# Second edge sort of a graph network kernel: one fp32 product per edge column becomes two 16-bit products

## The reference, cut to what matters

```python
src = src[_o]; dst = dst[_o]                  # 50000 edges
x = x + _L0_gnn_ref(_layernorm(x, axis=-1), L0_gnn_W, src, dst, edge_weight)
# inside: h = einsum('nd,od->no', x, W); msgs = edge_val[:, None] * h[edge_col]
#         out = segment_sum(msgs, edge_row, num_segments=N_NODES)
```

## Time and profile before

| | |
|---|---|
| median of 3 runs | 6542.18 us (6538.23 to 6543.29) |
| profiled execution, first to last instruction (span) | 6540.4 us |
| profiled execution, own time | not listed apart from the span |
| phase "a" with the second sort | about 467 to 1027 us |
| PE / DVE / ACT / POOL busy over the span | 79% / 53% / 38% / 26% |
| mean granted TensorE clock | 0.884 |

### The profile page before, as it was taken

How to read it: one execution, slowest core, us unless ns; L and a number is a source line. 1 busy time by engine, 2 the same in 40 slices (tenths; PEclk the granted TensorE clock), 3 DMA queues, 4 the chain that set the end, 5 groups by cost and what they waited for, 6 DMA issues and landing times. The chain is left out here.

```text
span 6540.4 us, 90176 instructions
## 1 busy us (share of the span) xinstructions
PE 5198.6 (79%) x22747; PEld 3549.0 (54%) x22748; DVE 3445.6 (53%) x7515; ACT 2507.4 (38%) x5926; POOL 1683.8 (26%) x1619
## 2 busy tenths in 40 slices
PE   6939998999796999997999679494656666646886
PEld 3516664444485777766788557273323444333576
DVE  9837777877654444435000244514369899855111
ACT  7947774666321000001223100131355666531343
POOL 5877771000022000001011300045334444310012
PEclk9979998999898999998999889797757777778888
DMA  1113333333263222221156432075324444430055
GB/s 30 23 17 100 102 101 106 150 150 153 105 201 111 72 71 71 72 76 39 50 188 199 148 100 66 23 211 159 120 57 130 133 131 135 118 100 2 27 158 171
DMA packets 407400, 682.31 MB, mean 104 GB/s; under 512 B 72738, under 2 KB 304300, under 8 KB 406732
## 3 DMA queue, kind: packets, MB, share of 16 engines
q1 hardware_dynamic: 328540, 489.55, 23.4%
q0 software_dynamic: 74192, 186.38, 10.5%
q10 hardware_dynamic: 4512, 4.46, 0.2%
HBM read 510.90 MB, written 169.02 MB: 104 GB/s over the span
## 5 line engine op out<-in xcount | busy, mean ns | idle before, releaser
L1683 POOL DMA_INDIRECT e_xb<-table,source x188 | 180.7, 961 | 2351.1 <-issue 1894.4
L1099 DVE TENSOR_TENSOR a_diff<-a_cu 128x640 f32<-128x640 uint16 x480 | 396.0, 825 | 627.5 <-PE a_pa L1137 627.5
L995 PE MATMUL ty_pc<-ty_ohr,ty_ohl 128*128 128x512 bf16 (+1 forms) x3416 | 662.5, 357 | 2.5 <-DVE ty_ohl L934 2.5
L2570 POOL DMA_INDIRECT mx_at_rows<-heads,mx_at_ix x416 | 483.1, 1161 | 622.3 <-PE mx_at_pa L2616 519.0
L1137 PE MATMUL a_pa<-a_diff,y_sb 128*128 128x320 f32 (+1 forms) x2000 | 548.4, 434 | 63.8 <-DVE a_diff L1106 63.8
L1640 ACT ACTIVATE e_h<-e_phid,e_b 128x256 f32<-128x256 f32 (+1 forms) x760 | 332.5, 438 | 688.0 <-PE e_phid L1598 670.2
L1661 DVE TENSOR_TENSOR e_ys<-e_py,e_bl 128x256 f32<-128x256 f32 x188 | 79.9, 425 | 968.3 <-PE e_py L1610 968.3
L969 ACT CAST ty_new<-ty_pc 128x512 uint16<-128x512 f32 x854 | 449.1, 541 | 266.6 <-PE ty_pc L995 266.6
L1598 PE MATMUL e_phid<-e_xt,e_w 128*128 128x256 f32 (+1 forms) x2800 | 524.0, 345 | 2.9 <-ACT e_xt L1628 2.9
L1610 PE MATMUL e_py<-e_wl,e_h 128*128 128x256 f32 x2288 | 512.4, 379 | 0.0
L995 PEld LDWEIGHTS ty_pc<-ty_ohr,ty_ohl 128*128 128x128 bf16 x3416 | 314.3, 98 | 350.7 <-DVE ty_ohl L934 4.2
(11 more groups left out here) (599 smaller groups left out, 8947.5 us busy)
## 6 DMA issues: line engine op xcount, KB each, us to landing
counts<-ty_snap SPq DMA_DIRECT2D x122, 800.0 KB
a_cu<-counts SPq DMA_DIRECT2D x500, 160.0 KB
mx_work<-bc SPq DMA_DIRECT2D x160, 320.0 KB, 3.6
e_w<-in_L_ffn_W SPq DMA_DIRECT2D x33, 1024.0 KB
e_wl<-in_L_ffn_W SPq DMA_DIRECT2D x32, 1024.0 KB
e_wl<-in_L_ffn_Wd SPq DMA_DIRECT2D x32, 1024.0 KB
ybuf<-e_ys POOLq DMA_DIRECT2D x78, 256.0 KB
e_w<-in_L_ffn_w SPq DMA_DIRECT2D x16, 1024.0 KB
```

Of the source, the lines that this page charges most:

```text
L995: mm = pe.matmul(pc[:, q, 0:w], ohl[:, h, j, ts(q, P)], ohr[:, h, j, 0:w], start=j == 0, stop=j == ROWS - 1)
L1099: v.tensor_tensor(diff[:, m % DIFFS, :], cu[:, s % R, :], cu[:, (s - 1) % R, :], ALU.subtract).then_inc(done, 1)
L2570: g.indirect_dma_start(self.rows[:, h * STEP + j, :], None, self.table, bass.IndirectOffsetOnAxis(ap=self.ix[:, h, j:j + 1], axis=0)).then ...
```

## The change

The value is split into its upper part (value >> 11) and its lower 11 bits, both whole numbers up to 2047. fp16 holds these exactly, so both one-hots become fp16 and each column has two 16-bit products in place of one fp32 product, into two PSUM banks. At the end the sums are joined again as upper * 2048 + lower. On DVE each column now has two hot instructions (q = 0, 1) of 125 x 128 with fp16 input and output in place of one in fp32. ACT's instructions keep their count and shape and write fp16. Before the first hots DVE makes a 16-bit iota and the pieces (five instructions, each behind the last), and `write` gains two instructions. In the diff `near` is the fp16 iota, `pieces` holds the two parts as fp32.

```diff
+    BITS = 11
+    SMALL = 1 << BITS
-        self.lanes, self.tiles = ph.sb("ss_lanes", [EP, 2, HALF, P]), ph.sb("ss_tiles", [EP, 2, HALF, ST])
+        self.lanes, self.tiles = ph.sb("ss_lanes", [EP, 2, HALF, 2, P], F16), ph.sb("ss_tiles", [EP, 2, HALF, ST], F16)
+        self.pieces, self.whole = ph.sb("ss_pieces", [EP, 2, EC + HALF]), ph.sb("ss_whole", [EP, 2, EC + HALF], I32)
-        self.sums = ph.ps("ss_sums", [P, 512])
+        self.sums = ph.ps("ss_sums", [P, 2, 512])
...
     def clear(self, v):
         v.memset(self.zero[:, :], 0.0).then_inc(self.cleared, 1)
+        self.c = c = Chain(v, self.chain)
+        whole, pieces = self.whole, self.pieces
+        v.tensor_copy(self.near[:, :], self.k.iota[0:EP, 0:P])
+        c(v.tensor_copy(whole[:, 0, :], self.k.edge_value[:, :]))
+        c(v.tensor_scalar(whole[:, 1, :], whole[:, 0, :], self.SMALL - 1, None, ALU.bitwise_and))
+        c(v.tensor_scalar(whole[:, 0, :], whole[:, 0, :], self.BITS, None, ALU.arith_shift_right))
+        c(v.tensor_copy(pieces[:, :, :], whole[:, :, :]))
...
     def lane_hots(self, v, m, b):
-            v.tensor_scalar(self.lanes[:, b, j, :], k.iota[0:EP, 0:P], k.edge_lane[:, ds(col, 1)], k.edge_value[:, ds(col, 1)],
-                            ALU.is_equal, ALU.mult).then_inc(self.hot, 1)
+            for q in range(2):
+                v.tensor_scalar(self.lanes[:, b, j, q, :], self.near[:, :], k.edge_lane[:, ds(col, 1)], self.pieces[:, q, ds(col, 1)],
+                                ALU.is_equal, ALU.mult).then_inc(self.hot, 1)
...
     def column(self, pe, m, b, j):
-        pe.wait_ge(self.hot, m * HALF + j + 1)
-        mm = pe.matmul(self.sums[:, 0:ST], self.lanes[:, b, j, :], self.tiles[:, b, j, :], start=False, stop=False)
+        for q in range(2):
+            pe.wait_ge(self.hot, (m * HALF + j) * 2 + q + 1)
+            mm = pe.matmul(self.sums[:, q, 0:ST], self.lanes[:, b, j, q, :], self.tiles[:, b, j, :], start=False, stop=False)
...
     def write(self, v):
+        c(v.tensor_copy(self.joined[:, :], self.sums[:, 1, 0:ST]))
+        c(v.scalar_tensor_tensor(self.joined[:, :], self.sums[:, 0, 0:ST], float(self.SMALL), self.joined[:, :], ALU.mult, ALU.add))
-        unpack(v, c, self.sums[:, 0:ST], self.row[:, :], self.none[:, :], self.lane[:, :], self.row_i[:, :], self.part[:, :])
+        unpack(v, c, self.joined[:, :], self.row[:, :], self.none[:, :], self.lane[:, :], self.row_i[:, :], self.part[:, :])
```

More of the change, by code:

```diff
@@ L192, in __init__ @@
             ph.sem("ss_" + n) for n in ("cleared", "hot", "away", "stood", "drawn", "listed", "chain", "passed"))
-        self.zero = ph.sb("ss_zero", [EP, ST], BF16)
-        self.lanes, self.tiles = ph.sb("ss_lanes", [EP, 2, HALF, P]), ph.sb("ss_tiles", [EP, 2, HALF, ST])
+        self.zero, self.near = ph.sb("ss_zero", [EP, ST], BF16), ph.sb("ss_near", [EP, P], F16)
+        self.lanes, self.tiles = ph.sb("ss_lanes", [EP, 2, HALF, 2, P], F16), ph.sb("ss_tiles", [EP, 2, HALF, ST], F16)
+        self.pieces, self.whole = ph.sb("ss_pieces", [EP, 2, EC + HALF]), ph.sb("ss_whole", [EP, 2, EC + HALF], I32)
+        self.joined = ph.sb("ss_joined", [P, ST])
         self.row, self.none, self.lane = (ph.sb("ss_" + n, [P, ST]) for n in ("row", "none", "lane"))
         self.row_i, self.part = ph.sb("ss_row_i", [P, ST], I32), ph.sb("ss_part", [P, ST], I32)
-        self.sums = ph.ps("ss_sums", [P, 512])
+        self.sums = ph.ps("ss_sums", [P, 2, 512])
     def clear(self, v):
         v.memset(self.zero[:, :], 0.0).then_inc(self.cleared, 1)
+        self.c = c = Chain(v, self.chain)
[5 more added lines that the diff above has]
+        c(v.tensor_copy(pieces[:, :, :], whole[:, :, :]))
     def begin(self, pe):
         pe.wait_ge(self.cleared, 1)
-        pe.matmul(self.sums[:, 0:ST], self.zero[:, 0:P], self.zero[:, :], start=True, stop=False).then_inc(self.drawn, 2)
+        pe.matmul(self.sums[:, 0, 0:ST], self.zero[:, 0:P], self.zero[:, :], start=True, stop=False)
+        pe.matmul(self.sums[:, 1, 0:ST], self.zero[:, 0:P], self.zero[:, :], start=True, stop=False).then_inc(self.drawn, 2)
     def lane_hots(self, v, m, b):
@@ L239, in end @@
     def end(self, pe):
-        pe.matmul(self.sums[:, 0:ST], self.zero[:, 0:P], self.zero[:, :], start=False, stop=True).then_inc(self.listed, 1)
+        pe.matmul(self.sums[:, 0, 0:ST], self.zero[:, 0:P], self.zero[:, :], start=False, stop=True)
+        pe.matmul(self.sums[:, 1, 0:ST], self.zero[:, 0:P], self.zero[:, :], start=False, stop=True).then_inc(self.listed, 1)
     def write(self, v):
-        c = Chain(v, self.chain)
+        c = self.c
         gi, kl, _, _ = self.lists
```

## The result

The changed kernel takes 6689.04 us (median of 4 runs, 6688.37 to 6690.39) against 6541.23 before (4 runs). The ratio is 1.0226, 95% interval 1.0212 to 1.0241: 148 us slower. 6673 was forecast, in a range of 6580 to 6710.

A forecast was written before the change was run, and what follows sets the result against it. DVE's chain, with waits for PE, was taken to set the half (eight columns), though PE was busiest. 50 halves x 2.5 plus 5.5 for the ends gave +130 us on 6542.2: 6672, stated as 6673, range 6580 to 6710.

The forecast's parts named there:

- The bound: Second sort: DVE's chain with its waits for PE fills 10.36 of a half's (eight columns') 10.49 us.
- Price of a 16-bit hot: DVE's lane hots: 0.222 us each in place of 0.256, 16 instead of 8, +1.50 us a half.
- The half at full clock: Second sort with PE's clock not falling: a half of 11.36 us, +0.87, or +43 us over 50 halves.
- PE's relief: PE's cheaper products free 2.8 us a half, of which at most 0.5 us can shorten the half.
- The gap and the clock: PE stands 4.1 us in one piece every half; its clock falls there and it returns at 1.2 GHz.
- the signs: Expected in the profile after: PE busy near 65%, clock 0.6 to 0.8, DVE waiting in the fifth to eighth additions.
- The size of the clock's price: Additions waiting for slow PE: +1.65 us a half, taken between +1.0 and +2.1, making a half 13.0 us.
- my upper case: PE at 1.2 GHz throughout: a half of 13.5 us, with PE no longer standing, so the clock would come back.
- The ends: Outside the repeated halves: preparing instructions 2.2, first hot group 1.5, `write` 0.9, round 26 1; some +5.5 us.
- Round 26: Part of the ends: the round starts at the low clock, +1 us.

The follow-up runs named there:

- With the clock held: Idle PE products after each half's fourth column: 20 against the changed kernel, 6592.3 us; 14 against the kernel before with every fp32 hot built twice, 6644.1 us.
- With eight hots and the clock let go: Changed kernel with only the upper piece's hots built, 8 instead of 16 a half, both products reading them, no idle products: 6536.5 us.

## Why the prediction was right

- *The bound.* That DVE's chain sets the half, at a busy share of 74%, held. With the clock held, eight more fp32 hots (2.05 us) lengthened it by 2.04. The 16-bit hots, 1.55 us more, lengthened it by 1.01, the additions being 0.43 shorter (the sum would be 1.12).
- *Price of a 16-bit hot.* 0.222 us was put together from other forms; 0.225 was measured. The Trainium skill's figure (VectorE: DVE Perf Modes, "Side-by-side: where the cycles go for N=2048 bf16"), 0.198 by my estimate, is too low here; the trace decides. Its shape, a large fixed part, is right.
- *The half at full clock.* 11.36 forecast, 11.50 measured with the clock held; +43 us forecast for 50 halves, 51 measured with the ends.
- *PE's relief.* Right: 0.5 us a half at most was forecast, and the additions took 0.43 less with the clock held. With eight hots and the clock let go, the whole gain was 4.7 us in the kernel, cheaper hots included.
- *The gap and the clock.* A gap of 4.1 us in every half was forecast; it is 4.1 (205.0 / 50), and the clock falls in it or, three times, just behind it. The rule of the Trainium skill (TensorE: Matmul & The Clock Gate, "HAM oscillation — how this bites in real kernels") is borne out, by removal too: closing the gap gives 97 us back. Of the signs, PE's busy share was 71% instead of near 65%, and the last three additions of a half wait for PE, not the last four.
- *The size of the clock's price.* This term was too small: +1.65 us a half forecast, +2.1 measured where the clock is low through the additions (6.54 instead of 4.40), +1.94 in the mean (13.44 less 11.50). I took a mean over places where the clock might come back. In the trace it comes back only as the eighth column is under way, in nearly every half, which is my upper case: 13.5 forecast for it, 13.44 measured. I had argued that in this case PE would no longer stand. It does: the clock comes back just in time for the next four columns, PE makes them at 0.80 us each and stands again. A half of 13.44 instead of 13.0 makes 22 us, 15 of them from the clock and 7 from the half at full clock. The total missed by only 16, since the ends were forecast 3.5 too high and the other stages came out 2.5 shorter.
- *The ends.* +5.5 forecast, about 2 measured: of the 149 us of the phase 147 lie in the 50 halves. The first hots start 2.1 us after the zeros are written (477.7 to 479.8), but before the change DVE waited for PE there and it was 0.9 (475.6 to 476.5), so the preparing instructions cost 1.2. The first group of hots added 1.6, and `write` 0.8, as forecast. Round 26 had the wrong sign: +1 was forecast for the low clock, and from the last addition of the round before to its own last index copy it took 17.8 us (1154.1 to 1171.9) instead of 19.8 (1001.4 to 1021.2).

What I did not see is that the fault is one of place: I priced the hots as time that nothing hides, and they were hidden almost wholly as soon as they stood between the additions, for 0.15 us a column.

## What to carry to other kernels

Lay each engine's work into one period, with its waits on itself, before relieving the engine with the highest busy share: here DVE, POOL and PE needed 9.9, 10.0 and 9.2 us of a half of 10.5, and taking 30% of its work from the busiest, PE, was worth under 0.1%, cheaper hots included. Work that is cheaper on one engine and doubled on another goes where that other engine waits anyway; ahead of a run that frees buffers it costs its full length, and a second time if it starves TensorE so long that its clock falls. After a change that leaves TensorE with time to spare, look at the granted clock of the stretch, and at whether TensorE stands in one long gap or in many short ones.

## What the runs showed of the hardware that I had not expected

- The clock settles into step with the loop. In the changed kernel it was low for some 6 us from each restart of PE, and back when the additions were nearly done, over and over, so the price was near its maximum in nearly every half and not spread between its bounds.
- Idle products cost nothing where they fitted into the gap: 3.68 us of them a half, 97 us gained. With eight, 63 us were gained, and no single length of the gap divides quick returns from slow ones: PE came back at full speed after 3.65 us without work in one half and slow after 2.40 in another.
- A two-pointer `tensor_scalar` of 128 elements costs 0.256 us in fp32 and 0.225 in 16 bit from start to start. Halving the width of the data saved 12% of the instruction.
